# Four edits to a graph-network kernel: pieces of P in fixed banks, reciprocals turned by transposes, fewer comparisons in the setup, masked loop ends

## The reference

```python
h = relu(layernorm(x)); x = x + L0(h)   # segment_sum of h[src] over dst, two dense layers, layernorm
h = relu(layernorm(x)); x = x + L1(h)   # attention along edges, 8 heads of 64, then a feed-forward layer
h = relu(layernorm(x)); x = x + L2(h)   # edge-weighted sums in both directions, dense, layernorm
h = relu(layernorm(x)); x = x + L3(h)   # mean over edges, two dense layers
# inside L1, the part that the change touches:
e = einsum('ehd,ehd->eh', k[src], q[dst]) / sqrt(64)
ex = exp(e - segment_max(e, dst)[dst]); attn = ex / segment_sum(ex, dst)[dst]
a = segment_sum(attn[:, :, None] * v[src], dst)
```

## Time and profile before

| | |
|---|---|
| median of 3 runs | 1137.26 us (1133.63 to 1137.53) |
| span of the profiled execution | 1133.4 us, mean granted clock 0.981 |
| TensorE busy (matmul) | 1052.5 us, 93% |
| VectorE busy | 583.0 us, 51% |
| ScalarE busy | 445.4 us, 39% |
| GpSimd busy | 157.7 us, 14% |

### The profile page before, as it was taken

One profiled execution on the slowest core, in us unless ns is written; L12 is line 12 of the kernel. 1 busy time (PEld: TensorE's weight loads), 2 busy tenths in 40 slices (PEclk: granted clock), 3 DMA queues, 4 the chain that ended last, 5 costly groups with the idle time before them and its releaser, 6 DMA issues.

```text
span 1133.4 us, 16827 instructions
## 1 busy us (share of the span) xinstructions
PE 1052.5 (93%) x5904; PEld 689.2 (61%) x5904; DVE 583.0 (51%) x1743; ACT 445.4 (39%) x762; POOL 157.7 (14%) x182
## 2 busy tenths in 40 slices
PE   6988878899999999899999999999899998999998
PEld 3456656555444554677777777774456896555443
DVE  7888998610884011666665666655447337300133
ACT  6502565400645101565555656552436415410000
POOL 0000000000053000333333000005537012000000
PEclk9999998899999999999999999999999999999999
DMA  5003788850100000554544100026001051100010
GB/s 169 1 0 106 221 259 269 261 178 1 40 35 1 19 19 31 177 152 150 152 140 144 42 1 1 2 82 245 0 1 47 1 192 36 38 1 1 10 46 35
DMA packets 73097, 93.63 MB, mean 83 GB/s; under 512 B 7169, under 2 KB 63176, under 8 KB 73022
## 3 DMA queue, kind: packets, MB, share of 16 engines
q1 hardware_dynamic: 73022, 92.62, 26.1%
HBM read 58.00 MB, written 34.60 MB: 82 GB/s over the span
## 4 chain that ended last, share of the span: by engine, by line
PE 79%; DVE 10%; issue 5%; ACT 4%; DMA 1%; SPq 1%; DVEq 0%; ACTq 0%
PE PS L557 8%; PE PS L788 8%; PE PS L590 8%; PE PS L771 8%; PE PS L936 7%; PE PS L743 7%; PE PS L971 6%; PE PS L714 5%; PE PS L613 5%; PE PS L529 2%; DVE R L1241 2%; PE PS L700 2%; DVE HT L1106 2%; PE PS L891 2%; PE PS L918 2%
## 5 line engine op out<-in xcount | busy, mean ns | idle before, releaser
L557 PE MATMUL PS<-HT,R 125*128 125x313 bf16 x636 | 130.5, 351 | 27.0 <-DVE HT L1106 15.8
L1230 DVE CUSTOM_DVE_ANT_0 HT<-PS,CD 128x1250 f32<-128x1250 f32 (+1 forms) x80 | 116.4, 1455 | 67.4 <-issue 67.4
L557 PEld LDWEIGHTS PS<-HT,R 125*128 x636 | 98.0, 172 | 59.9 <-issue 45.4
L771 PE MATMUL PS<-K,HT 128*128 128x128 f32 (+2 forms) x800 | 112.5, 280 | 15.0 <-DVE R L1241 14.4
L1535 ACT COPY R<-PS 128x512 f32<-128x512 f32 (+1 forms) x120 | 64.8, 574 | 121.5 <-PE PS L771 119.5
L1555 ACT ACTIVATE HT<-HT,soft 128x1250 f32<-128x1250 f32 (+1 forms) x80 | 107.1, 1338 | 10.3 <-DVE soft L1233 3.3
L771 PEld LDWEIGHTS PS<-K,HT 128*128 128x128 f32 (+2 forms) x800 | 84.0, 140 | 43.2 <-DVE R L1241 23.6
L743 PE MATMUL PS<-R 64*128 64x512 f32 (+3 forms) x480 | 95.8, 531 | 3.1 <-DVE soft L1230 3.1
L788 PE MATMUL PS<-R 128*64 128x128 f32 (+2 forms) x1600 | 94.2, 273 | 0.0
L788 PEld LDWEIGHTS PS<-R 128*64 128x64 f32 (+1 forms) x1600 | 84.8, 137 | 6.4 <-issue 5.8
L590 PE MATMUL PS<-CD,H 128*128 128x512 f32 (+2 forms) x240 | 86.0, 520 | 2.4 <-ACT X L1445 2.4
(11 more groups left out here) (222 smaller groups left out, 1386.2 us busy)
## 6 DMA issues: line engine op xcount, KB each, us to landing
edge_parts<-X SPq DMA_DIRECT2D x160, 156.5 KB, 2.7
R<-edge_parts SPq DMA_DIRECT2D x60, 156.5 KB, 2.3
CD<-edge_sums SPq DMA_DIRECT2D x1, 6250.0 KB, 20.8
CD<-edge_parts SPq DMA_DIRECT2D x10, 469.5 KB, 3.8
BC<-edge_parts SPq DMA_DIRECT2D x30, 156.5 KB, 2.5
CD<-edge_parts SPq DMA_DIRECT2D x3, 1565.0 KB, 10.8
edge_sums<-R SPq DMA_DIRECT2D x20, 156.5 KB, 2.8
R<-edge_parts SPq DMA_DIRECT2D x18, 155.5 KB, 2.3
```

Source lines behind the costliest of these rows:

```text
L557: return mm(bank(b0 + h, QUART), stat, hot, start=first, stop=True, skip_group_check=True)
L771: m = nc.tensor.transpose(PS[0:rows(j), o:o + n], Pb[u % 2][a][0:n, j * P:j * P + rows(j)], ident[0:n, 0:n])
L1230: ve.tensor_tensor_reduce(Pb[s][a][0:n], PS[0:n, a * N:(a + 1) * N], cd[0:n, t, :], 1.0, -3e38, ALU.add, ALU.max, soft[0:n, s, a:a + 1]).t ...
```

## The change

Four edits:

- **Pieces of P in fixed banks.** Piece i of every unit goes to bank 6, 7, 6, 7, 4. Pieces 2 and 3 wait for pieces 0 and 1 of the same unit to be copied out, pieces 0 and 1 for pieces 2 and 3 of the unit before. Piece 4 lies in a bank of the scores: it waits for both maxima of unit u+1, and the fifth matmul of the scores of unit u+2 waits for its copy.
- **Reciprocals by transposes.** VectorE writes each reciprocal times `hasedge` 64 times over into `rzw` (128x256), and two transposes take the place of four products with `ident`.
- **Setup.** One comparison for each direction and half in place of two in turn, none linked to the next, and the matrices of `chunk_rows` in float32r, for which VectorE copies the ones once more.
- **Loop ends masked.** The loop end read from the table goes through `& ENDS` (16383) in a register.

```diff
+PIECE_BANK = (6, 7, 6, 7, 4)
+ENDS = 16383
...
-                     v[VALUES * k + GH].with_bounds(min_val=w + k + 2, max_val=(w + k + 1) * (NC - FIX) + 1))
+                     (v[VALUES * k + GH] & ENDS).with_bounds(min_val=w + k + 2, max_val=(w + k + 1) * (NC - FIX) + 1))
...
-                mm(bank(4)[0:NW, 0:NC], K1[0:80, K_ONES:K_ONES + NW], diag[:, 0:4, :], start=True, stop=True)
+                mm(bank(4)[0:NW, 0:NC], ones_r[0:80, 0:NW], diag[:, 0:4, :], start=True, stop=True)
...
                         if (j, a) == (2, 0):
                             pe.wait_ge(sem("s_half"), u + 1)
+                            if u >= 2:
+                                piece_out(PIECES * (u - 1) - 1)
...
-                if c >= 2:
+                if i >= 2 and i < 4:
                     piece_out(c - 2)
+                elif i < 2 and u > 0:
+                    piece_out(c - PIECES + 2)
+                elif i == 4 and u + 1 < UNITS:
+                    pe.wait_ge(sem("s_max"), 2 * u + 4)
...
-                        o = (6 + c % 2) * BANK + (2 * jj + a) * P
+                        o = PIECE_BANK[i] * BANK + (2 * jj + a) * P
...
                 for b in range(2):
-                    for a in range(2):
-                        o = RZ + b * P
-                        i = mm(PS[a * DK:(a + 1) * DK, o:o + n],
-                               rz[0:n, 2 * b + a:2 * b + a + 1].to_broadcast([n, DK]), ident[0:n, 0:n], start=True,
-                               stop=True, skip_group_check=True)
+                    i = nc.tensor.transpose(PS[:, RZ + b * P:RZ + b * P + n], rzw[0:n, b * P:(b + 1) * P], ident[0:n, 0:n])
...
+            ve.tensor_copy(ones_r[:, :], K1[:, K_ONES:K_ONES + P])
...
-                for q, k in ((0, K2_UP), (1, K2_DOWN)):
-                    link(ve.scalar_tensor_tensor(reach[:, q, :], last, K1[0:NW, K_TLO + h:K_TLO + h + 1], K2[:, k:k + NC],
-                                                 ALU.is_ge, ALU.mult))
-                    link(ve.scalar_tensor_tensor(span[:, q, h, :], first, K1[0:NW, K_THI + h:K_THI + h + 1],
-                                                 reach[:, q, :], ALU.is_le, ALU.mult))
+                ve.scalar_tensor_tensor(span[:, 0, h, :], first, K1[0:NW, K_THI + h:K_THI + h + 1],
+                                        K2[:, K2_UP:K2_UP + NC], ALU.is_le, ALU.mult)
+                i = ve.scalar_tensor_tensor(span[:, 1, h, :], last, K1[0:NW, K_TLO + h:K_TLO + h + 1],
+                                            K2[:, K2_DOWN:K2_DOWN + NC], ALU.is_ge, ALU.mult)
+            link(i)
...
-                    ve.tensor_scalar(rz[0:n], rz[0:n], hasedge[0:n, t:t + 1], None, ALU.mult).then_inc(sem("z_ready"), 1)
+                    ve.tensor_scalar(rzw[0:n].rearrange("p (h d) -> p h d", d=DK), rz[0:n].unsqueeze(2).to_broadcast([n, 4, DK]),
+                                     hasedge[0:n, t:t + 1], None, ALU.mult).then_inc(sem("z_ready"), 1)
...
-                                       bank(6 + c % 2).rearrange("p (j n) -> p j n", j=4)[:, :, 0:n])\
+                                       bank(PIECE_BANK[i]).rearrange("p (j n) -> p j n", j=4)[:, :, 0:n])\
```

More of the change, by code:

```diff
@@ L21 @@
 BF16 = mybir.dt.bfloat16
+F32R = mybir.dt.float32r
 I32 = mybir.dt.int32
@@ L118, in build @@
         X = sb("X", [P, T, D])
+        cd_at = nc.sbuf_base
         CD = sb("CD", [P, T * N])
+        diag_r = nc.alloc_sbuf_tensor_at("diag_r", [P, 640], F32R, offset=cd_at)
+        ones_r = nc.alloc_sbuf_tensor_at("ones_r", [P, P], F32R, offset=cd_at + 4 * 5400)
         R0 = sb("R0", [P, 20992])
@@ L191, in build @@
         dext = HT[0:80, 4840:4848]
-        diag = CD[0:80, 0:640].rearrange("p (a e) -> p a e", a=8)
+        diag = diag_r[0:80, :].rearrange("p (a e) -> p a e", a=8)
         K2 = CD[0:NW, 640:640 + NK2]
-        reach = CD[0:NW, 1400:2040].rearrange("p (q c) -> p q c", q=2)
         span = CD[0:NW, 2040:3320].rearrange("p (q h c) -> p q h c", q=2, h=2)
@@ L217, in build @@
         rzb = BC[:, 0:2 * P].rearrange("p (b n) -> p b n", b=2)
+        rzw = BC[:, 1200:1200 + 4 * DK]
         ybuf1 = R0[:, 5120:5120 + 4 * D].rearrange("p (s o) -> p s o", s=4)
@@ L463, in chunk_rows @@
                 pe.wait_ge(sem("setup_dve"), 1)
-                mm(bank(4)[0:NW, 0:NC], K1[0:80, K_ONES:K_ONES + NW], diag[:, 0:4, :], start=True, stop=True)
-                mm(bank(2)[0:NW, 0:NC], K1[0:80, K_ONES:K_ONES + NW], diag[:, 4:8, :], start=True, stop=True).then_inc(sem("setup_ps"), 1)
+                mm(bank(4)[0:NW, 0:NC], ones_r[0:80, 0:NW], diag[:, 0:4, :], start=True, stop=True)
+                mm(bank(2)[0:NW, 0:NC], ones_r[0:80, 0:NW], diag[:, 4:8, :], start=True, stop=True).then_inc(sem("setup_ps"), 1)
             def weight_shift():
@@ L1535, in piece @@
                 sc.copy(PT[c % RING].rearrange("p (j n) -> p j n", j=4)[:, :, 0:n],
-                        bank(6 + c % 2).rearrange("p (j n) -> p j n", j=4)[:, :, 0:n]).then_inc(sem("pt_act"), 1)
+                        bank(PIECE_BANK[i]).rearrange("p (j n) -> p j n", j=4)[:, :, 0:n]).then_inc(sem("pt_act"), 1)
             def spread(v):
```

## The result

| | before | after |
|---|---|---|
| median | 1136.33 us, 4 runs (1133.63 to 1137.53) | 1109.02 us, 4 runs (1108.24 to 1110.02) |
| ratio | | 0.9769, 95% interval 0.9752 to 0.9787 |
| span of the profiled execution | 1133.4 us | 1107.4 us |
| mean granted clock | 0.981 | 0.983 |

So the direction was right and a size was not.

What follows compares the result with a forecast made beforehand. TensorE, busy 93% of the span, was taken as the bound. Stall -16.8, reciprocals -3.6, setup 0 and masks +2.4 summed to -18.0 us, from 1137.26 to 1119.3 us, range 1113 to 1131.

Steps and rivals of the forecast that it cites:

- The stall went, and nothing took its place: Attention: piece 4's wait for VectorE's copy leaves the wait list, and no line in the scores replaces it.
- the cover: Attention: piece 4's copy ends 0.36 us before the fifth score matmul's weight load, so that wait costs nothing.
- What a stall costs: Attention: piece 4's wait for piece 2's copy costs 0.42 us in each of 40 units, 16.8 us gained.
- refilling of the weight path: Attention: the part of the 0.42 us stall beyond the 0.35 us shown as idle.
- cover of pieces 0 and 1: Attention: their wait for pieces 2 and 3 is covered; piece 3's copy ends at 501.92, needed at 503.84 us.
- Reciprocals: Attention, every second unit: two transposes at 0.26 us replace products at 0.44 us, 3.6 us gained over 20.
- Setup: Setup: VectorE gets about 2.3 us ahead, hidden because TensorE is busy from 24 us; cost 0.
- Masks: Window loop: one engine's instruction exposed at 39 jumps back, two more at ten table reloads; +2.4 us.
- Fully in series: Window loop: all mask instructions exposed on both engines, 8.9 us; as a rival 1125.8 us, chance 0.07.
- The clock's rival: Attention: TensorE's clock falls with transposes standing together; 1177 us if one unit in five falls, chance 0.03.

Runs made afterwards that it cites:

- e7_wait_first: Changed kernel with the wait for piece 4's copy moved from the fifth score matmul to the first; 1144.5 us, ratio 1.0080 to the kernel before.
- e8_wait_third: Changed kernel with the wait for piece 4's copy moved from the fifth score matmul to the third; 1124.53 us, ratio 0.9906 to the kernel before.
- e1_banks: Kernel before with only the masked loop ends and the pieces in fixed banks; 1114.68 us, ratio 0.9823 to the kernel before.
- e2_recips: Kernel before with only the masked loop ends and the reciprocals by transposes; 1132.97 us, ratio 0.9985 to the kernel before.
- e5_old_setup: Changed kernel with the setup of before put back; 1110.85 us, ratio 0.9796 to the kernel before.
- e3_masks: Kernel before with the masked loop ends alone; 1137.22 us, ratio 1.0018 to the kernel before.
- e10_mask_each: Changed kernel with each loop end masked once, in its own register ahead of its loop, none in a pass; 1109.19 us, ratio 0.9771 to the kernel before.
- e6_copy_wait: Changed kernel with piece 4 in bank 4 but again waiting for the copy of piece 2; 1134.62 us, ratio 0.9995 to the kernel before.

## Why the prediction was right in kind and wrong in size

- **The stall went, and nothing took its place.** Right. The wait is gone from the list, TensorE is busy 240.00 of 240 us, and no row of the scores waits for VectorE's copy. e7_wait_first and e8_wait_third show that the cover was there and thin: 0.40 us in the trace after, put at 0.36.
- **What a stall costs: the step that failed.** The prediction said "The loss is 0.42 us, 0.35 of it shown as idle, the rest the refilling of the weight path", and made 16.8 us both its value and its upper bound ("at the most 16.8"). It measured 21.7 us (e1_banks against before), 0.57 a unit. Two readings of the earlier trace rows were wrong. First, "piece 4 could start at 501.02" takes eight transposes at 1.02 us. That is the distance to the weighing, whose first product starts 0.20 us after the last transpose (497.46 to 497.66), where a transpose that follows another starts 0.11 us after it. In a row the ninth starts after 0.93 us, so piece 4 could have started at 500.93, and 0.09 us of the wait were left out. Second, the loss ended where piece 4 starts, though its four transposes take 0.58 us behind the pause. The prediction's own cover of pieces 0 and 1 has 0.52 for them ("501.02 + 0.52 + 2.30"), but the 0.06 us between the two were not charged. 0.42 + 0.09 + 0.06 = 0.57, and 38 units of that are 21.7. No run shows a refilling of the weight path in the 0.42 us: the 0.07 us that it stood for lie between 501.02 and 501.09, the modelled end of the eighth transpose, where idle time begins to count. The first unit, ahead of the third scores, gave 0.8 us more: those start 13.8 us into the attention in e1_banks, of which 4.54 - 2.37 = 2.17 are its slow second scores, so 11.6, and 12.4 in e2_recips, which has the stall and 2.37 us of second scores.
- **Reciprocals.** Forecast 3.6, measured 4.0 (e2_recips); 0.22 us a pair remain where 0.26 were taken from the earlier trace rows. Right; the 0.26 come from the same 1.02 us, and two steps of 0.11 us are the 0.22.
- **Setup.** Forecast 0, measured nothing (e5_old_setup). Right that it is hidden, but not where the prediction looked for the cover: the 2.3 us lead ends in the wait for TensorE at 28 us (3.77 us in place of 0.95), and the 3.29 us at the second window step never saw it.
- **Masks.** Forecast +2.4. The nine window loops with masks in the passes have a mean of 162.2 us, 2.4 above before's one trace, and e3_masks is 2.0 slower by medians. Of the 39 jumps back (79 passes in 40 groups) 24 lie in the first group, so the term has 24 x 0.04 = 1.0 us there; 1.26 us are measured, about one engine's mask a pass. It has 0.6 + 0.8 = 1.4 us for the other 39 groups, and 1.1 us (0 to 2) remain there. That part is a guess that happened to fit: the nine kernels scatter over 2 us in it, no run shows masks exposed at the reloads, and e10_mask_each, with no mask in a pass, loses 2.3 us there. "Fully in series" (8.9) was far off. The Trainium skill, "Advanced Engine Details and Errata", section "Engine Queue Depths", gives VectorE a queue of 8 entries. The prediction drew from it that by this alone all masks would be hidden; in the first group they are not, by 1.2 to 1.3 us in nine kernels of nine.
- **The clock's rival.** False: the attention holds 1.00 with twelve transposes in a row and no pause at all. The Trainium skill, "TensorE: Matmul & The Clock Gate", "Part 4: PE-mode transpose", says that the full clock does not engage for transposes. The trace does not agree: 1.00 over 240 us with 20 or more transposes in each unit.
- **The sum.** Measured terms: -21.7 - 0.8 - 4.0 + 2.4 = -24.1 us. The profiled executions differ by 26.0; the other 1.9 are the clock at the second scores (-1.0) and in the aggregation (-1.7), the start (+0.5) and 0.3 of scatter in the window loop. By medians it is 27.3 us with an interval, from the ratio, of 24 to 28.
- **The range.** Its low end was 16.8 + 3.6 and the luck of one low run. Its stall term ended at 16.8 us, with no room for 0.57 us a unit. With 21.7 in its place that end would lie near 1108, and the result inside; so one undersized bound put it outside. The clock at the second scores and in the aggregation, 2.7 us between the two traces, was not in the sum either.

## What to carry to other kernels

Measure what a stall costs from the start of one undisturbed unit to the next, and never as the idle time a row shows: here 0.35 us of idle were 0.57 us of time. Most of the rest, 0.16 us, is hidden by the row itself: a matmul's record lasts 0.27 us, the next one in a row starts 0.11 us after it, and idle time begins to count only when the record ends. To find the part that isn't shown, compare the start of the same instruction in a full row and behind the pause. Don't take a row's length from its first instruction to the next kind of work: the change to other work takes longer than the step to one more of the same. When a buffer is moved to a place with another owner, count the slack up to the weight load of the instruction that waits, not up to its matmul.

## What the runs showed of the hardware

- 128x128 f32 transposes in a row start 0.11 us apart (after, 497.84 to 497.95). From the last of eight to the first product of the weighing it is 0.20 us (before, 497.46 to 497.66), and the first transpose behind other work or behind the pause in before takes 0.17 us to the next (after 497.02 to 497.19, before 501.44 to 501.60); behind the longer pause of e6_copy_wait it takes 0.14 us. The clock was 1.00 in both.
- A pause shown as 0.35 us of idle cost 0.57 us (before against e1_banks), one of 0.44 us cost 0.64 us (e6_copy_wait against after).
- A wait in the middle of a row of matmuls costs time that no TensorE row shows as idle: 0.37 us a unit in e8_wait_third, visible only as 0.55 us before a weight load.
- After a pause of 3.15 us of TensorE, the clock of what follows differed, with no cause that these runs show: the same twelve score matmuls took 2.37, 3.35 or 4.54 us (granted clock 1.00, 0.69 and 0.50), and 2.37 and 3.2 us in two executions of the same kernel. One such place is worth up to 2.2 us, as much as a whole term of this sum, so single traces of a stage must not be compared across it.
- One register instruction more on each engine (40 ns on VectorE, 36 ns on TensorE) in the first group's loop, where the two answer each other, costs 0.05 us a pass (25.98 to 27.24 us for 25 passes).
